# A gated cross-attention decoder on one core: the second attention's softmax sum taken once per head, inverted small and spread by TensorE, with newly written engine orders

## What the reference computes

```python
scores = jnp.einsum('bhqd,bhkd->bhqk', q, k) * scale
attn = jax.nn.softmax(scores, axis=-1)
out = jnp.einsum('bhqk,bhkd->bhqd', attn, v)
out = out.transpose(0, 2, 1, 3).reshape(B, Lq, DIM)
return out @ Wo.T + bo
```

## Time and profile before

| what | value |
|---|---|
| median of 3 runs | 265.4 us (265.31 to 266.64) |
| the profiled execution, whole | 264.35 us |
| its span, first to last instruction | 262.4 us |
| TensorE (PE) busy | 254.0 us, 97% |
| VectorE (DVE) busy | 217.1 us, 83% |
| ScalarE (ACT) busy | 192.2 us, 73% |
| GpSimd (POOL) busy | 31.1 us, 12% |

### The profile page before, as it was taken

The page is one execution under the profiler, slowest core; times in us unless marked ns, Lnnn a source line. Parts: engine busy times, 40 slices in busy tenths (PEclk is TensorE's granted clock), DMA queues, the critical chain, the costliest instruction groups (busy, mean ns, idle before and its releaser), DMA issues.

```text
span 262.4 us, 5607 instructions
## 1 busy us (share of the span) xinstructions
PE 254.0 (97%) x1869; PEld 189.2 (72%) x1869; DVE 217.1 (83%) x534; ACT 192.2 (73%) x463; POOL 31.1 (12%) x53
## 2 busy tenths in 40 slices
PE   7899999999999999999999999989999999999996
PEld 3568779779779878868787788767657565575675
DVE  5599979866766698998999787889899999899861
ACT  1689887788658678697899966179998699834551
POOL 3000002000000010201100102020003110424130
PEclk9999999999999999999999999999999999999999
DMA  6293491300400004300300000000000000000001
GB/s 184 56 239 97 95 343 32 90 4 0 95 1 1 2 0 101 86 0 4 92 4 0 0 2 0 4 0 1 2 0 4 4 1 0 2 9 4 21 10 40
DMA packets 8848, 10.70 MB, mean 41 GB/s; under 512 B 1115, under 2 KB 5877, under 8 KB 8821
## 3 DMA queue, kind: packets, MB, share of 16 engines
q1 hardware_dynamic: 7792, 9.70, 13.7%
q10 hardware_dynamic: 1029, 0.65, 0.8%
HBM read 4.99 MB, written 0.52 MB: 21 GB/s over the span
## 4 chain that ended last, share of the span: by engine, by line
PE 70%; DVE 18%; ACT 5%; issue 5%; POOL 1%; DVEq 0%; ACTq 0%; POOLq 0%
PE slot L518 19%; PE slot L608 13%; PE slot L589 6%; PE slot L590 6%; PE slot L564 3%; PE slot L615 3%; DVE mx L1152 3%; PE slot L570 2%; PE slot L761 2%; PE slot L755 2%; DVE RB L1157 2%; ACT S L910 2%; PE slot L706 2%; PE slot L749 2%; PE slot L579 2%
## 5 line engine op out<-in xcount | busy, mean ns | idle before, releaser
L1046 DVE TENSOR_REDUCE nm<-slot 128x1 f32<-128x589 f32 x64 | 47.6, 766 | 9.7 <-PE slot L590 9.3
L838 ACT ACTIVATE PR<-slot,nm 128x589 f32<-128x589 f32 x64 | 47.7, 749 | 9.3 <-DVE nm L1046 8.8
L518 PE MATMUL slot<-K,PR 128*128 128x128 f32 (+1 forms) x320 | 44.3, 276 | 0.2
L589 PE MATMUL slot<-KH,Q 128*128 128x296 f32 (+1 forms) x128 | 42.1, 345 | 0.2
L518 PEld LDWEIGHTS slot<-K,PR 128*128 128x128 f32 (+1 forms) x320 | 36.1, 142 | 8.1 <-ACT PR L838 5.0
L608 PE MATMUL slot<-PT,V 128*64 128x256 f32 (+1 forms) x320 | 38.1, 384 | 0.7 <-ACT PT L773 0.7
L773 ACT ACTIVATE PT<-slot 128x640 f32<-128x640 f32 x47 | 32.2, 705 | 8.3 <-PE slot L518 7.3
L590 PE MATMUL slot<-KL,Q 128*128 128x296 f32 (+1 forms) x128 | 36.1, 299 | 0.0
L910 ACT ACTIVATE S<-slot,mx 128x77 f32<-128x77 f32 x128 | 29.2, 365 | 6.3 <-DVE mx L1152 5.6
L608 PEld LDWEIGHTS slot<-PT,V 128*64 128x64 f32 (+1 forms) x320 | 22.1, 137 | 12.3 <-issue 3.5
L589 PEld LDWEIGHTS slot<-KH,Q 128*128 128x128 f32 x128 | 24.2, 189 | 3.6 <-issue 1.4
(11 more groups left out here) (169 smaller groups left out, 478.2 us busy)
## 6 DMA issues: line engine op xcount, KB each, us to landing
KH<-KH SPq DMA_DIRECT2D x16, 147.5 KB, 2.5
KL<-KL SPq DMA_DIRECT2D x16, 147.5 KB, 2.6
CTT<-in_ctxT SPq DMA_DIRECT2D x1, 640.0 KB, 3.9
K<-in_const SPq DMA_DIRECT2D x1, 589.0 KB, 4.9
WGU<-in_wgu SPq DMA_DIRECT2D x1, 580.0 KB, 6.0
out<-X SPq DMA_DIRECT2D x8, 64.0 KB, 1.5
L1W<-in_l1w SPq DMA_DIRECT2D x1, 384.0 KB, 3.8
WD<-in_wdT SPq DMA_DIRECT2D x1, 320.0 KB, 6.5
```

What stands on the lines that cost most here:

```text
L518: return pe.transpose(dst, src, ident[0:p, 0:p])
L589: pe.matmul(W[:, K0 + lo:K0 + hi], q, KH[:, g % 4, lo:hi], start=True, stop=False)
L838: act.activation(PR[:, s, :], W[:, K0:K0 + KEYS0], ACT.Exp, bias=nm0[:, s:s + 1], accum_out=sum0[:, b, p * 2 + f, t, e:e + 1]).then_inc(pr ...
L1046: dve.tensor_reduce(nm0[:, s:s + 1], W[:, K0:K0 + KEYS0], AX.X, ALU.max, negate=True).then_inc(max_ready, 1)
```

## The change

The second attention's sums are formed once per head. On TensorE the 12 matmuls with `vmask` are replaced by 40: for each of the 10 chunks of `PT1` and each quarter of 64 queries, 32 weight columns (`summask`) against 64 queries, the quarter's number choosing the group of 32 columns. The 16 heads' sums of 256 queries then lie in 128x64 (each head twice). VectorE inverts 128x64. A new TensorE stage, T, spreads the inverses over the heads' rows with 4 matmuls of 128 weight columns (`spread`) against 64 columns, back into the 256 columns of the bank. ScalarE copies them to `RB1` (new stage A1 of `a6`), and VectorE multiplies in a stage of its own (D2; the former D2 and D3 become D3 and D4). The masks are built once: three memsets and five copies in `a3` of batch 0, one transpose on TensorE and four copies of 32x128 in `a3` of batch 1.

`PLAN` is written anew. The number of words of each kind stays, but for those of `a6`. Fillers fall from 85 to 10. Of the copies of `a4`, VectorE had 2 of 16 and gets 6; of `f3`, 4 of 8 and gets 5; of `u`, 17 of 64 and gets 15; ScalarE has the rest.

The core of the diff (of `PLAN` the lines around the last `a6`; the lines for `m2` and `m4` in VectorE's second stage are only moved):

```diff
 PLAN = """
...
-m2:D2 m2:B m2:A2 m4:B a6:D3 m1:F6 a6:B m4:D2 m2:P1 m2:D1 m2:D2 m4:F0 m1:A1 m3:F2 m2:F6 a6:D2 a6:P2 m2:A1 m2:F4 m4:A1 m3:D1 m2:B m3:A1 m2:P1
-m2:A2 m4:B m2:A1 m2:B+2@3 m3:D2 m4:D2 m2:P1 a6:D3 m4:F0 m2:D1 m2:A2 m2:D2 m2:D1 m2:F2 m4:A1 m2:D2 m2:B m2:A1 m1:F6 m2:A2 m1:A1 m4:B m2:P1 m2:D1
...
...
+m2:A2 m2:F4 m3:A1 m2:B m4:A1 a6:D4 m2:A1 m3:D2 m4:B m1:F2 a6:D1 m2:P1 m2:A2 a1:P1 m2:D1 m2:D2 m4:D2 m2:D1 a6:T m1:A1 m4:F0 m4:A1 m2:D2 a6:A1
+m3:F2 m3:D1 m2:F6 m3:A1 m2:F4 a6:D2 m4:B m2:A1 m3:D2 m4:D2 m2:P1 a6:B m2:B m4:F0 a6:D3 m2:A2 m2:B a6:P2 m2:F2 m4:A1 m2:A1 m2:B m2:D1 m2:D2
...
 """
...
+        summask = sb("summask", [P, 2, KC1, 32])
+        spread = sb("spread", [P, 4, P])
+        inverse = sb("inverse", [P, N // 4])
...
                 elif kind == "a3":
+                    if b == 1:
+                        pe.wait_ge(masks_ready, 1)
+                        turn(W[:, 7 * P:8 * P], RB1[:, 0:P])
...
                             mm = pe.matmul(W[g * 32:(g + 1) * 32, 0:N], V1[:, b, g, i, :], pt,
                                            start=(i == 0), stop=(i == GC - 1))
-                    for i in range(GC):
-                        for g in range(G1):
-                            pt = PT1[:, part % 2, g // 2 * KC1 + g % 2 * 2 + i, :]
-                            mm = pe.matmul(W[g * 32:(g + 1) * 32, N:2 * N], vmask[:, g % 2, i].rearrange("p h d -> p (h d)"),
-                                           pt, start=(i == 0), stop=(i == GC - 1))
+                    pe.wait_ge(masks_ready, 1)
+                    for c in range(2 * KC1):
+                        for g in range(4):
+                            mm = pe.matmul(W[g * 32:(g + 1) * 32, N:N + N // 4], summask[:, c // KC1, c % KC1, :],
+                                           PT1[:, part % 2, c, g * N // 4:(g + 1) * N // 4],
+                                           start=(c == 0), stop=(c == 2 * KC1 - 1))
                 elif kind == "m1":
...
+            def widen(item):
+
+                W = slot(item)
+                warm(item, "T")
+                pe.wait_ge(sum1_inverted, upto(item))
+                pe.wait_ge(spread_ready, 4)
+                for g in range(4):
+                    mm = pe.matmul(W[:, N + g * N // 4:N + (g + 1) * N // 4], spread[:, g, :], inverse[:], start=True, stop=True)
+                mm.then_inc(inverse_spread, 1)
 
...
-            walk("PE", {"F": front, "B": back})
+            walk("PE", {"F": front, "T": widen, "B": back})
...
+                elif kind == "a6":
+                    act.wait_ge(inverse_spread, n)
+                    if n == 1:
+                        act.wait_ge(cn_ready, B)
+                    if n > 1:
+                        act.wait_ge(a1t_ready, n - 1)
+                    act.activation(RB1[:], W[:, N:2 * N], ACT.Copy).then_inc(rb1_ready, 1)
...
+                        link_all([dve.memset(summask[:], 0.0), dve.memset(RB1[:, 0:P], 0.0), dve.memset(spread[:], 0.0)])
+                        link_all([dve.tensor_copy(summask[:, h, :, r:r + HH], blocks) for h in range(2) for r in (h * HH, H1 + h * HH)])
+                        link(dve.tensor_copy(RB1[:, 0:P].rearrange("p (g h) -> p g h", h=32)[:, :, 0:H1], K[:, K_MASK:K_MASK + H1].unsqueeze(1).broadcast_to([P, 4, H1])))
...
                     if n > 1:
                         dve.wait_ge(k1_ready, n - 1)
+                        for g in range(4):
+                            rows = slice(g * 32, (g + 1) * 32)
+                            dve.tensor_copy(spread[rows, g, :], W[rows, 7 * P:8 * P]).then_inc(spread_ready, 1)
...
                 elif kind == "a6":
 
-                    if n > 2:
-                        dve.wait_ge(ya_done, n - 2)
-                    link(dve.reciprocal(RB1[:], W[:, N:2 * N]))
-                    dve.tensor_tensor(A1T[:, item[2] * N:(item[2] + 1) * N], W[:, 0:N], RB1[:],
-                                      ALU.mult).then_inc(a1t_ready, 1)
+                    if n > 1:
+                        dve.wait_ge(inverse_spread, n - 1)
+                    dve.reciprocal(inverse[:], W[:, N:N + N // 4]).then_inc(sum1_inverted, 1)
...
                 elif kind == "a6":
+                    dve.wait_ge(rb1_ready, n)
+                    if n > 2:
+                        dve.wait_ge(ya_done, n - 2)
+                    dve.tensor_tensor(A1T[:, item[2] * N:(item[2] + 1) * N], W[:, 0:N], RB1[:],
+                                      ALU.mult).then_inc(a1t_ready, 1)
...
+            def third(item):
+                kind, b, n = item[0], item[1], upto(item)
+                if kind == "a6":
+                    W = slot(item)
...
+            def fourth(item):
+                n = upto(item)
+                dve.wait_ge(rstd_ready[3], n)
+                for m in range(part_tiles(item).start, part_tiles(item).stop):
+                    normalise(3, X3, m, XN[:, m, :], xn_ready[3])
...
-            walk("DVE", {"D0": early, "D1": first, "D2": second, "D3": third, "C": copy})
+            walk("DVE", {"D0": early, "D1": first, "D2": second, "D3": third, "D4": fourth, "C": copy})
```

More of the change, by code:

```diff
@@ L134 @@
[L134 to L137 removed]
+x0:F2 x0:A1 k:F0 k:A1 q:F7 k:D1 q:A1 k:F2 k:A1 v:F4 v:Ca q:D1 v:F0 k:D1 u:F6 u:F2 u:F4 u:D1 u:D1 v:Ca u:D1 u:A1 u:F0 u:D1
@@ new lines @@
+u:A1 u:B u:B u:A1 u:Ca u:B u:A1 u:F6 s:D2 u:B u:Ca u:Cd u:F4 u:Ca u:F2 u:D1 q:F0 s:F1 u:A1 u:D1 u:D1 s:D1 w:D0 u:A1
+u:B u:A1 u:B u:Ca u:Ca v:F1 k:F6 w:P1 u:F4 v:Ca q:A1 k:A1 q:D1 k:D1 u:D1 u:B w:F1 u:Ca u:F6 u:F2 w:A1 w:D1 u:A1 u:B
+u:F0 u:D1 u:A1 u:D1 u:Cd u:B u:F4 w:D0 u:A1 u:D1 u:Ca u:B u:Cd u:D1 u:A1 u:F6 u:D1 w:P1 u:B u:A1 q:F3 u:Ca q:A1 w:D0
+u:A1 x0:D2 q:D1 w:F2 w:A1 w:D1 u:B u:B u:F0 u:Ca u:Ca u:D1 u:F4 w:P1 u:D1 u:F6 u:A1 u:D1 u:A1 u:A1 a3:F2 u:B u:B u:Ca
+u:Ca u:B u:Ca a3:D1 x0:P2 u:F0 k:F4 w:F7 w:D0 k:A1 k:D1 w:P1 u:F2 u:D1 u:D1 w:A1 u:F4 u:A1 q:F6 u:D1 u:B u:A1 u:B w:D1
@@ new lines @@
+u:A1 u:Cd g:F7 u:B u:Ca u:Ca u:F0 q:A1 x0:D3 u:F2 g:D1 u:F4 w:F7 u:D1 u:A1 u:B u:D1 q:D1 u:A1 u:D1 u:B w:A1 u:A1 u:Ca
+w:D1 u:Cd u:F6 w:D0 u:B u:Ca u:F0 u:D1 u:D1 u:A1 x0:F2 a3:F4 u:A1 a3:D1 x0:A1 w:P1 u:B u:Ca u:B a3:P1 k:F2 u:F6 u:Ca u:F0
+u:D1 k:A1 u:D1 k:D1 u:A1 w:D0 w:F4 u:A1 w:A1 w:P1 u:B w:D1 q:F2 u:Cd u:F4 u:F6 u:D1 q:A1 u:B u:D1 u:A1 u:A1 u:Ca w:D0
+w:F3 w:A1 q:D1 u:B u:B w:D1 u:Ca w:P1 u:F0 u:D1 u:Ca u:F4 u:A1 w:F7 u:D1 u:B u:A1 u:F2 w:A1 w:D1 u:B o:F6 u:Ca u:F0
+u:D1 u:A1 o:D1 u:D1 u:B u:F6 u:Ca u:F4 u:Ca u:D1 u:A1 u:A1 o:F3 u:B u:D1 u:B u:Cd u:A1 q:F2 u:F0 o:D1 u:B u:Ca w:D0
@@ L138 @@
+m4:B m4:D2 m4:B m4:D2
 """
@@ L351, in mega_kernel @@
         a1t_ready = sem("a1t_ready")
+        spread_ready = sem("spread_ready")
+        sum1_inverted = sem("sum1_inverted")
+        inverse_spread = sem("inverse_spread")
+        rb1_ready = sem("rb1_ready")
         ya_done = sem("ya_done")
@@ L1254, in third @@
             def third(item):
-                kind, n = item[0], upto(item)
-                if kind == "x0":
+                kind, b, n = item[0], item[1], upto(item)
+                if kind == "a6":
+                    W = slot(item)
+                    r = part_tiles(item)
+                    dve.wait_ge(ya_done, n)
+                    dve.wait_ge(x2b_ready, n)
+                    dve.scalar_tensor_tensor(out=X3[:, r, :], in0=W[:, N:N + TP * D].rearrange("p (t d) -> p t d", t=TP),
+                                             scalar=tg[:, 1:2], in1=X3[:, r, :], op0=ALU.mult,
+                                             op1=ALU.add).then_inc(x3_ready, 1)
+                    dve.wait_ge(x3_ready, n)
+                    all_stats(3, X3, r)
+                    variance(3, r)
+                elif kind == "x0":
                     dve.wait_ge(rstd_ready[0], PARTS + 1)
@@ L1280, in third @@
                         normalise(2, X2, m, XN[:, m, :], xn_ready[2])
-                elif kind == "a6":
-                    dve.wait_ge(rstd_ready[3], n)
-                    for m in range(part_tiles(item).start, part_tiles(item).stop):
-                        normalise(3, X3, m, XN[:, m, :], xn_ready[3])
+            def fourth(item):
[3 more added lines that the diff above has]
+                    normalise(3, X3, m, XN[:, m, :], xn_ready[3])
             def copy(item):
                 {"u": copy_turned, "a4": copy_turned1, "v": copy_values, "f3": copy_quantised}[item[0]](dve, "DVE", item)
-            walk("DVE", {"D0": early, "D1": first, "D2": second, "D3": third, "C": copy})
+            walk("DVE", {"D0": early, "D1": first, "D2": second, "D3": third, "D4": fourth, "C": copy})
 def constants():
```

66 lines of the change are left out of this document (23 added, 43 removed).

## The result

The changed kernel takes 266.74 us, median of 20 runs (265.92 to 267.88), the kernel before 265.4 us in 20 runs of the same kind: a ratio of 1.0052 with a 95% interval of [1.0037, 1.0067]. It is half a per cent slower, where half a per cent faster was forecast. The profiled execution took 266.44 us with a span of 264.6, against 262.4 before, so the sum to explain is +2.2 us of span.

The account below looks back on a forecast made before the run. TensorE was taken to bound to 160 us and in the tail, VectorE between, to about 243. Terms -0.6 - 1.4 + 0.3 - 0.1 + 0.35 = -1.4 us, off the 265.4 median, gave 264.0 us; range 262.4 to 267.2.

Parts of the forecast that it names:

- VectorE, -0.6: VectorE from 160 to 242.85 us: smaller reciprocals save 4.8 us, but added copies and products leave net -0.6 us.
- rival 5: From 160 to 175 us the new order closes another microsecond of VectorE's and ScalarE's waits: 262.7 us, chance 0.14.
- TensorE, the sums: no change: The 80 sum instructions at each `a6` front take 1.3 us, as before, with 1.1 and 4.8 as ends.
- Rivals 2 and 3: Sums' narrow matmuls paced by number: starts 30 ns apart, 265.5 us, chance 0.08; or costlier, 267.5 us likelier, chance 0.12.
- TensorE, the spread: Four spreads of 0.9 us, +3.6 in all; padding covers the first two, the last two charged 0.35, ends 0 and 1.8.
- rival 1: VectorE's net relief is only 0.6 us and spreads cost a full 1.8 where TensorE is full: about 265.4 us, chance 0.14.
- The last `m1`, -1.4: Between the last `a6` back and `m1`, four TensorE words instead of ten, so VectorE sets that point: -1.4 us.
- Tail fillers, +0.3: Behind the last `m1`, four fillers in three places, of which three count at 0.11 us: +0.3 us.
- The first 160 us, -0.1: TensorE has one transpose more and two fillers fewer, -0.1 us; VectorE's masks charged 0, possibly up to 1 us.
- Rival 4, the clock: Without fillers between 165 and 206 us, TensorE runs at 1.2 GHz for 5 us; 2.5 us outlast slack: 266.5 us, chance 0.05.

Follow-up runs that it names:

- the one with fourteen fillers: Kernel after the change with 14 fillers ahead of the first `f2` of batch 1 and no others added: 264.75 us, ratio 0.9986 to the kernel before.
- the version with the shift alone: Kernel after the change with five start-up matmuls of 512 columns replaced by twelve of 213, moving later TensorE instructions some 28 places: 266.06 us, ratio 1.0031.
- the fp32r version: Kernel after the change with inverses and spread weights held as fp32r, each spread matmul one instruction instead of two: 264.9 us, ratio 0.9973 to the kernel before.
- the fp32r version with fillers and shift: Kernel after the change with fp32r spreads, fourteen fillers ahead of an `f2`, and twelve start-up matmuls for five: 265.37 us, ratio 0.9986 to the kernel before.

## Why the prediction was wrong

The bound was named for the wrong stretch. The prediction let VectorE set the pace from 175 to about 243 us, though its own rows gave TensorE 24.11 of 24.57 us from the end of the third front on the earlier trace rows. There each TensorE instruction that is added is paid for. Point by point:

- **VectorE, -0.6.** The reciprocal took 0.557 us, forecast 0.56. Up to the third front the kernel gained 1.2 us, somewhat more than was charged; rival 5 had seen that possibility. The 1.2 us are what is left after the half clock took its share there, and no run separates the two.
- **TensorE, the sums: no change.** Right in kind, and a little better: 1.23 us instead of 1.43, so -0.2 each and -0.4 in the full stretch. 1.08 us from first to last start is at the lower end that was given, 1.1, the pace of the columns. The Trainium skill's floor ("TensorE: Matmul & The Clock Gate", section "Wait — 56ns, not 53.3ns?": never below about 25 ns from start to start) does not hold in this trace, which has 13.7 ns with four groups of columns side by side. Rivals 2 and 3, which rested on a pace by number, are refuted for the sums.
- **TensorE, the spread: the step that failed.** Its size was right (0.9 forecast, 0.84 measured). "I charge 0.35 as an estimate, and keep 0 and 1.8": the upper end was true, 2 x 0.84 = 1.7 us. The cover that I named, VectorE bringing the third front earlier, can't exist: an earlier start does not shorten a stretch in which TensorE is full. This is rival 1's mechanism, which I gave 0.14. With the hole shifted away the full stretch has 28.55 us, 1.27 more than before, and 1.68 for the spreads less 0.40 for the sums make 1.28.
- **The last `m1`, -1.4: the second step that failed.** Its first half is right, though the new order has five words of TensorE there and not the four that I counted (`m2:B m4:F0 m2:B m2:F2 m2:B`): with five instead of ten behind the last `a6` back, `m1` starts as soon as its normalise has run. But I counted words only from that back on. From the third front to the last `m1` `PLAN` has 30 of TensorE's words before and 33 after: 31 and the two spreads. The five words that left the place behind the last back stand ahead of it, with the spreads and an `m3` front, so the back came later (241.38 instead of 235.02) and the normalise with it (245.00 instead of 241.81 - 0.6). In a full stretch a move gains nothing: the 1.27 us above leave no room for a gain of 1.4. The run with the last `a6` moved forward agrees as far as it goes, since its product came earlier and the kernel did not get faster; but it has waits of its own.
- **Not foreseen: the hole**, 0.94 us. Nothing in the profile of before hinted at it, since that kernel has no burst of this kind.
- **Tail fillers, +0.3:** 18.41 against 18.13 us, and 18.15 without them. Right.
- **The first 160 us, -0.1:** +0.3 from the first to the last `u` maximum, within the microsecond that was allowed. Whether it is the masks is open, since no run has the new orders without them. In the old orders they were not covered: the run with the old orders and the new sums lost 2.2 us there.
- **Rival 4, the clock.** It happened (0.05 was too little for that), and its price was too high: I had 2.5 us of doubled work outlasting the slack. Between the kernel after and the one with fourteen fillers, 6.8 us of half clock moved the third front by 0.1 us; in the trace of the kernel before without its fillers, 10.24 us moved it by 1.2.

In the full stretch the terms add up: 1.68 for the spreads, 0.94 for the hole, -0.40 for the sums make +2.22; measured +2.21. This leaves the `m3` front that stands there in addition, some 0.4 us, against small differences in pauses and hand-overs, which I have not separated.

With the steps mended in the prediction's own sum, -1.2 up to the third front, +2.2 in the full stretch, +0.3 in the tail and +0.3 in the first attention make +1.6 us against a forecast of -1.4.

Why did the version with the shift alone stay at 1.0031 when the one with fourteen fillers reached 0.9986, and both have 28.55 us in the full stretch? Their intervals touch at 1.0007 to 1.0013, and most of it is how the executions fell. The times of these kernels lie in two groups about a microsecond apart, which the mean granted clock of the execution tells apart. Of the shifted version five executions (clock 0.981) have a median of 265.15 us and seven (0.974) of 266.48, so the median of all fell into the upper group. With fourteen fillers seven (0.987) have 264.65 and five (0.994) 265.77, so it fell into the lower one. Like with like they differ by 0.5 to 0.7 us. Of the kernel after, eight (0.980 or 0.981) have 266.2 and twelve (0.974) 266.92: against it the shift gained 1.05 and 0.44 us. In the fp32r version the same shift, which brings the hole back, cost 1.3 us in the lower group (264.2 to 265.46) and 0.7 in the upper one (265.52 to 266.24). The hole's price in the traces, 0.94 and 0.96 us, lies between these.

What stays open: the 0.5 to 0.7 us that remain between those two versions, how much of the -1.2 us up to the third front the half clock took, and the 0.3 us of the first attention. The best version is the fp32r spread, 0.9973 [0.9952, 0.9994]; by the result above, part of that hangs on where its instructions happen to lie.

## What to carry to other kernels

Before an added instruction is charged below its length, find out per stretch whether its engine ever idles there: in a full stretch charge all of it, and give nothing for moving words about inside the stretch, counting them from where it becomes full and not from the last dependence. A dense burst of tiny matmuls can outrun the loading of its own instructions: look for a pause put down to "issue" inside the burst with a packet of the instruction queue beside it, and shift the stream by a few dozen instructions to test it. When two medians of a dozen executions differ by a microsecond or so here, compare them group by group. If an edit gains or loses more than the work that it changes, compare the stretches of the two traces before giving it a cause; fourteen fillers "repaired the clock" here and in truth moved a hole.

## What the runs showed of the hardware

- **Instruction loading can stall TensorE.** A burst is 160 records in about 1.08 us, 6.8 ns apiece. In the kernel after, the transfer of a 16 KB block starts at 229.87 us and the stalled burst goes on at 232.21, 2.3 us later; over the six kernels with a hole this is 2.3 to 2.6 us, and the hole in TensorE's rows 0.62 to 0.96 us. Where the same load began well before the burst (227.03 for one whose first record is at 229.73), there was none, nor where the burst was over before the record at which the others stall (a load at 228.86, a burst at 228.93 of 160 records from 3837 on). That TensorE had used up what was loaded when it came to record 4029 is my reading of this pattern; no record shows what was loaded or when a block is asked for.
- **Narrow fp32 matmuls in four column groups** start 13.7 ns apart with 64 columns each, for 79 steps on end, weight loads included.
- **Fillers of constant transposes keep the clock up, and it was worth little here.** Before: clock 1.00 with them, 10.24 us at half without, for 0.2% [-0.1%, 0.45%] in the runs and 1.2 us in the trace. It depends on what the low clock falls on. In the profile of the fp32r version with fillers and shift it reached the first `a6` front, whose 24 matmuls then took 2.79 us instead of 1.50, and the third front came 57.9 us behind the last `u` maximum instead of 56.6.

```profile
190.55 2.79 PE L695 MATMUL slot<-PT,V 128*32 128x256 f32 x24
```

- **The start is a lottery of a microsecond.** The first `u` maximum comes at 15.7 to 17.1 us in the profiled executions, and the tail does not make up for it. The two groups of executions go with it where no fillers were added: the traces with a mean clock of 0.98 have it at 15.7 to 16.3 us and 10.24 us of half clock, those with 0.972 to 0.974 at 16.5 to 17.1 us and 13.65 us of half clock. The kernel before has the groups without any half clock to speak of: on one chip 19 executions with a mean clock of 1.000 have a median of 264.86 us, 16 with 0.998 or 0.999 one of 265.8.
